# Slot selectors of a routing table: eight wide comparisons on VectorE in place of 64 narrow ones on GpSimd

## Chip, cores and metric

The kernel runs on one core of a Trainium2 chip. The metric is the device time of one execution in microseconds (us); for the kernel before, three runs gave 2314.49, 2322.72 and 2324.0 us, so the median is 2322.72 us.

## The reference

Input x has 4096 tokens of 256 features, all float32. Two layers follow each other; each adds an attention-like part and a routed feed-forward part to the stream, both fed by the same layer norm:

```python
x = L0_attn_x
xn = _layernorm(x, axis=-1)
x = x + _L0_attn_ref(xn, ...) + _L0_ffn_ref(xn, ...)
xn = _layernorm(x, axis=-1)
x = x + _L1_attn_ref(xn, ...) + _L1_ffn_ref(xn, ...)
```

The change touches the second layer, in the stage that does its attention and the routing of its feed-forward part. The feed-forward part has 8 experts, and each token goes to the 2 with the highest scores, weighted by a softmax over the two:

```python
scores = jnp.einsum('bsd,ed->bse', x, Wg)
topk_scores, topk_idx = jax.lax.top_k(scores, k)
topk_probs = jax.nn.softmax(topk_scores, axis=-1)
h1 = jnp.einsum('bsd,efd->bsef', x, W1)
h2 = jnp.einsum('bsd,efd->bsef', x, W2)
hidden = jax.nn.silu(h1) * h2
expert_out = jnp.einsum('bsef,edf->bsed', hidden, W3)
...
return jnp.einsum('bse,bsed->bsd', gating, expert_out)
```

The attention part of that layer projects xn to q, k and v, normalizes each over all tokens (batch norm), takes a steep sigmoid of each, forms the 16x16 products v'v of each head, and multiplies q*k by them and by an output matrix.

## The kernel before

The program is a row of stages, each a block in which all engines have an instruction list of their own, with semaphores between them; at a block's end the engines meet. The stages are: the first norm, routing and state-space attention of layer 0, the experts of layer 0, the stage between the layers (`bridge_phase`, from line 1501), and the experts of layer 1 (`expert_phase`, called on line 2158). The last needs the lists that `bridge_phase` makes: for each of 72 tiles of 128 slots, sorted by expert, the token of each slot (`source`, `target`) and its weight (`gate`).

These lists are made by matrix products, without a scatter. There are 32 x 2 = 64 pairs of a token tile and a choice. For a pair, each of 128 tokens (on the partitions) has a tile `tile_f` (0 to 71) and a slot in that tile `slot_f` (0 to 127). The product of a 128x128 selector (1 where the column number is the token's slot) with a 128x144 load (token number, and weight, in the column of the token's tile) adds the tokens into the 128x144 `table`. The pairs are handled in 8 batches (`BATCHES`) of 8 pairs (`EB`). Selectors (`pick`) and loads (`loads`) have two buffers each, used in turn.

Who does what, and in which order:

- GpSimd makes the selectors in a loop at the end of its list (lines 1655 to 1663): eight comparisons of `slot_row` (0 to 127 along the columns) with one column of `slot_f` per batch, each 128x128. From batch 2 on it waits until the batch two before is multiplied (`s_tab`), and after each batch it raises `s_pick`.
- VectorE makes the loads in `load(m)` (lines 1953 to 1964) by three operations on 128x576 elements (lines 1959, 1962, 1964), each of which waits for the one ahead. `load(0)` and `load(1)` stand ahead of the loop, on both sides of `coefficients(0, K, 1)`, and `load(n + 2)` stands in step n of `v_step` (lines 1993 to 2008), for n from 0 to 5.
- TensorE's `v_step(n)` (lines 1733 to 1758): eight transposes of v (line 1740), in steps 0 and 1 also two more units of the projections (line 1674), then the wait for `s_pick` and `s_load`, the eight table products (line 1749), the wait for VectorE's copies of the transposed v (`s_vk`), and the eight v'v products (line 1756). Float32 matrix products stand twice in the profile's counts (x16 for eight).
- VectorE's `v_step(n)`: wait for the transposes, two copies out of PSUM (line 1997), in steps 0 to 3 four `bn_stats` (line 1870), in step 4 `moments` (lines 1969 to 1971), then `load(n + 2)`, an addition of a bias to the stream (line 2006), and in step 5 `coefficients(K, R, 2)` (lines 1977 to 1982), for which ScalarE waits before the sigmoids of k.
- ScalarE does the sigmoids (line 1831), of v, then q, then k.

After eight steps VectorE masks the v'v products (line 2013), TensorE forms the effective output matrix (line 1763), and the output loop (lines 1774, 2025, 2043) follows; then the experts begin. The expert stage gathers rows by `source` on GpSimd's queue (line 1286).

In the names of the rows below, `b_work` and `b_xn` are areas that several arrays share: the selectors lie in `b_work`, the loads of even batches in `b_work` and of odd ones in `b_xn`, and `tile_f`, `slot_f` in `b_xn`. `b_bank` is PSUM.

Of the kernel before, what the change touches and what calls it, by code (L numbers as in the profile page):

```python
# [7 lines left out]
ALU = mybir.AluOpType  # L8
# [4 lines left out]
P = 128  # L13
# [100 lines left out]
def bcast(ap, n):  # L114

    return ap.unsqueeze(2).to_broadcast([ap.shape[0], ap.shape[1], n])
# [1384 lines left out]
def bridge_phase(nc, sem, k, xs, y_dram, xnT, rows, w_small, w_qkv, w_p, bn_g, bn_b, bp, lists, etab, etab_dram, out, s_out, w13s, w2s):  # L1501
# [11 lines left out]
    e_n, k_n, nt = E1, K1, NT1  # L1513
    by_token = y_dram[SPARE:SPARE + S * K0, :].rearrange("(s k) d -> s (k d)", k=K0)
    with ctx:
# [27 lines left out]
        tile_f, slot_f = (spare[:, o:o + T * k_n].rearrange("p (t q) -> p t q", q=k_n) for o in (384, 448))  # L1543
        live = spare[:, 512:512 + nt]
        source, aimed, gate = lists
        EB = 8
        pick = work[:, 4096:4096 + 2 * EB * P].rearrange("p (r e s) -> p r e s", r=2, e=EB)
        loads = [b.rearrange("p (e a j) -> p e a j", e=EB, a=2)
                 for b in (work[:, 6144:6144 + EB * 2 * nt], spare[:, 640:640 + EB * 2 * nt])]
        slot_row_i, slot_row = sb("slot_row_i", [P, P], I32), sb("slot_row", [P, P])  # L1550
# [29 lines left out]
        s_rc, s_sel, s_pre, s_e, s_ex, s_rt = (sem("b_" + n) for n in (  # L1580
            "route_chain", "selected", "counted", "exp_in", "exp_out", "routed"))
        s_cz, s_iota, s_turn, s_pick, s_load, s_tab, s_et, s_etm = (sem("b_" + n) for n in (
            "comparisons_zeroed", "iotas", "iotas_turned", "slots_picked", "loads_set", "tabled", "expert_of_tile", "expert_moved"))
# [7 lines left out]
        BATCHES = T * k_n // EB  # L1591
# [8 lines left out]
        with nc.Block() as block:  # L1600
            @block.sync
            def _(sp):
                def y_half(h):
                    g, half = divmod(h, 2)
                    if g >= 2:
                        sp.wait_ge(s_x, g - 1)
                    sp.dma_start(yg[:, g % 2, half * 2:half * 2 + 2].rearrange("p t k d -> p t (k d)"),
                                 tokens(by_token, g * BIG + half * 2, 2)).then_inc(s_yg[h % 4], 16)

                for h in range(4):  # L1610
                    y_half(h)
                for g in range(NG):
                    if g + 2 < NG:
                        y_half(2 * g + 4)
                        y_half(2 * g + 5)
                    sp.wait_ge(s_xn, g + 1)
                    sp.dma_start(tokens(rows, g * BIG, BIG), xn[:, g % XN]).then_inc(s_row[g % XN], 16)
                sp.wait_ge(s_et, 1)
                sp.dma_start(etab_dram.rearrange("(c p) -> p c", p=P), etab_i[:], allow_slow_non_contiguous=True).then_inc(s_etm, 16)
                sp.wait_ge(s_etm, 16)  # L1620
                sp.dma_start(etab[:], etab_dram[0:nt].unsqueeze(0)).then_inc(s_etm, 16)
                for g in range(NG):
                    sp.wait_ge(s_xo, g + 1)
                    sp.dma_start(tokens(out, g * BIG, BIG), xs[:, g * BIG:(g + 1) * BIG, :]).then_inc(s_out, 16)
                for r in range(XN):
                    sp.wait_ge(s_row[r], len(range(r, NG, XN)) * 16)
                sp.wait_ge(s_etm, 32)

            @block.gpsimd
            def _(pool):  # L1630
                g_ = nc.gpsimd
                for h in range(2 * NG):
                    g, half = divmod(h, 2)
                    pool.wait_ge(s_yg[h % 4], (h // 4 + 1) * 16)
                    a = yg[:, g % 2, half * 2:half * 2 + 2]
                    g_.tensor_tensor(a[:, :, 0:2, :], a[:, :, 0:2, :], a[:, :, 2:4, :], ALU.add).then_inc(s_pc, 1)
                    pool.wait_ge(s_pc, h + 1)
                    g_.tensor_tensor(a[:, :, 0, :], a[:, :, 0, :], a[:, :, 1, :], ALU.add).then_inc(s_ys, 1)
                    if h == 1:
                        g_.iota(tokid[:], pattern=[[P, T]], base=-S, channel_multiplier=1).then_inc(s_iota, 1)  # L1640
                        g_.iota(ji[:], pattern=[[1, 1]], base=0, channel_multiplier=1).then_inc(s_iota, 1)
                        g_.iota(slot_row_i[:], pattern=[[1, P]], base=0, channel_multiplier=0).then_inc(s_iota, 1)
                        pool.wait_ge(s_iota, 3)
                        g_.tensor_copy(token_f[:], tokid[:]).then_inc(s_turn, 1)
                        g_.tensor_copy(jf[:], ji[:]).then_inc(s_turn, 1)
                        g_.tensor_copy(slot_row[:], slot_row_i[:]).then_inc(s_turn, 1)
                pool.wait_ge(s_x, NG - 1)
                g_.memset(cmp, 0.0).then_inc(s_cz, 1)
                g_.memset(mask[:], 1.0).then_inc(s_m, 1)
                m3 = mask[:].rearrange("p (h d) -> p h d", d=HD)  # L1650
                for n, (op, low, sign) in enumerate(((ALU.is_ge, 0, 1), (ALU.is_ge, HD - 1, -1))):
                    pool.wait_ge(s_m, n + 1)
                    g_.affine_select(out=m3, in_=m3, compare_op=op, fill=0.0, base=low,
                                     pattern=[[-sign * HD, P // HD], [0, HD]], channel_multiplier=sign).then_inc(s_m, 1)
                pool.wait_ge(s_rt, 1)
                pool.wait_ge(s_turn, 3)
                for n in range(BATCHES):
                    if n >= 2:
                        pool.wait_ge(s_tab, n - 1)
                    for x in range(EB):  # L1660
                        t, q = divmod(n * EB + x, k_n)
                        ins = g_.tensor_scalar(pick[:, n % 2, x, :], slot_row[:], slot_f[:, t, q:q + 1], None, ALU.is_equal)
                    ins.then_inc(s_pick, 1)

            @block.tensor
            def _(pe):
                mm = nc.tensor.matmul
# [181 lines left out]
            def _(dve):  # L1849
                v = nc.vector  # L1850
# [72 lines left out]
                for e in range(e_n):  # L1923
                    ins = v.tensor_tensor_scan(incl[:, :, e], k["ones"][:, 0:T], tot[:, :, e], 0.0, ALU.mult, ALU.add)
# [28 lines left out]
                def load(m):  # L1953
                    at = slice(m * EB // k_n, (m + 1) * EB // k_n)
                    half = lambda a: loads[m % 2][:, :, a, :].rearrange("p (t q) j -> p t q j", q=k_n)
                    wide = lambda ap: ap.unsqueeze(3).to_broadcast([P, EB // k_n, k_n, nt])
                    if m >= 2:
                        dve.wait_ge(s_tab, m - 1)
                    v.tensor_tensor(half(0), slot_row[:, 0:nt].unsqueeze(1).unsqueeze(1).to_broadcast([P, EB // k_n, k_n, nt]),
                                    wide(tile_f[:, at, :]), ALU.is_equal).then_inc(s_load, 1)  # L1960
                    dve.wait_ge(s_load, 3 * m + 1)
                    v.tensor_tensor(half(1), half(0), wide(gates[:, at, :]), ALU.mult).then_inc(s_load, 1)
                    dve.wait_ge(s_load, 3 * m + 2)
                    v.tensor_tensor(half(0), half(0), wide(bcast(token_f[:, at], k_n)), ALU.mult).then_inc(s_load, 1)
# [20 lines left out]
                for n in AFTER[:8]:  # L1985
                    unit(n)
                moments(0, K, FULL)
                load(0)
                dve.wait_ge(s_nb, 4)
                coefficients(0, K, 1)  # L1990
                load(1)

                def v_step(s):
                    reached(dve, s_vt, s)
                    reached(dve, s_vv, s, 2)
                    for b in range(2):
                        ins = v.tensor_copy(vt[:, s.slot(2), 2 * b:2 * b + 2, :].rearrange("p u d -> p (u d)"), v_ps[b][:])
                    ins.then_inc(s_vk, 1)
                    for n in AFTER[8 + 4 * s.n:12 + 4 * s.n]:
                        unit(n)  # L2000
                    if s.n == 4:
                        moments(K, R, UNITS)
                    if s.n + 2 < BATCHES:
                        load(s.n + 2)
                    part = xs[:, s.n * BIG:(s.n + 1) * BIG, :]
                    v.tensor_tensor(part, part, middle(bp[:], BIG), ALU.add).then_inc(s_bp, 1)
                    if s.n == 5:
                        coefficients(K, R, 2)
# [3 lines left out]
                for c in range(KD):  # L2012
                    ins = v.scalar_tensor_tensor(vv[:, c, :], v_sum[c][:, 0:P], SCALE, mask[:], ALU.mult, ALU.mult)
# [15 lines left out]
                for c in range(KD):  # L2029
                    ins = v.tensor_copy(weff[:, c, :], bank[6 + c][:, 0:D])  # L2030
# [18 lines left out]
def program(nc, x, w_proj, b_proj, b_dt, conv_w, dt_bias, a_log, d_col, norm_col, w_out, b_out,  # L2049
# [11 lines left out]
    with ExitStack() as top:  # L2061
# [89 lines left out]
        with Semaphores(nc, sem) as own:  # L2151
            bridge_phase(nc, own, k, xs, y0, xnT, rows, wsm1, wqkv, wp, g_sb, b_sb, bp_sb, lists1, etab1, etabs[1], out, s_out, w13s, w2s)
# [49 lines left out]
```

## Time and profile before

| what | value |
|---|---|
| median of three runs | 2322.72 us (2314.49 to 2324.0) |
| time of the profiled execution | 2307.0 us |
| its span in the trace | 2305.1 us |
| mean granted TensorE clock | 0.985 |
| busy: TensorE / VectorE / ScalarE / GpSimd | 93% / 68% / 52% / 62% |
| the stage of the change, from the first copies of `v_step` to the last v'v product | 1777.58 to 1829.17 us, 51.6 us |
| GpSimd's selectors | 64 comparisons, first at 1758.8 us, last at 1824.5 us |

The profile is that of one execution, and its times are microseconds from the start of the span. A timeline row gives the start, the time to the end of its last instruction, engine, line, operation and tiles, the count, and in brackets how long the engine was idle ahead of it and what ended that. The time between two rows' starts is what an engine really takes for the first of them, since the end of one instruction overlaps the start of the next by a little (0.07 us on VectorE).

### The profile page before, as it was taken

To read this page: it belongs to the slowest core of one execution; us is meant where nothing else is said; L and a number is where in the kernel's file an instruction comes from. 1 tells how busy PE (TensorE), PEld (TensorE's weight loads), DVE (VectorE), ACT (ScalarE), POOL (GpSimd) and SP (SyncE) were. 2 spreads that over 40 slices of the span, in tenths; PEclk is the share of its full clock that TensorE was granted. 3 is DMA by queue.
4 is the path that set the end of the run, shared out by engine and by line. 5 is a ranking of instruction groups with operands and counts; after the bars stand their busy time and mean duration, and the time that the engine had idled before them with its cause. 6 is when DMAs were issued, how large, how long until landed. Compare 5 with 4: busy or idle time off the path is not lost. (4 is left out here: it accounts for less than half of the span.)

```text
span 2305.1 us, 40600 instructions
## 1 busy us (share of the span) xinstructions
PE 2152.2 (93%) x12292; PEld 1574.2 (68%) x12292; DVE 1572.4 (68%) x3391; ACT 1205.1 (52%) x2706; POOL 1439.0 (62%) x1272
## 2 busy tenths in 40 slices
PE   4878999999999999999999989999799889999997
PEld 2446777777777777777777768788444756666664
DVE  5778888888888888888888865677596832222221
ACT  2456777777777777777777752222254511111111
POOL 1325777777777777777777766788672624444443
PEclk9989999999999999999999999999899999999999
DMA  9864445555445455544554527976450064222221
GB/s 323 320 145 115 138 146 151 152 143 145 143 138 147 138 142 148 155 139 143 147 155 140 147 72 239 296 244 198 173 212 10 19 219 128 46 46 44 45 43 19
DMA packets 193826, 329.02 MB, mean 143 GB/s; under 512 B 49235, under 2 KB 135508, under 8 KB 193364
## 3 DMA queue, kind: packets, MB, share of 16 engines
q1 hardware_dynamic: 137220, 232.12, 34.1%
q0 software_dynamic: 26880, 53.64, 9.0%
q10 hardware_dynamic: 29520, 40.66, 5.5%
q8 instruction: 110, 1.80, 0.3%
q14 instruction: 96, 0.79, 0.1%
HBM read 240.46 MB, written 86.79 MB: 142 GB/s over the span
## 5 line engine op out<-in xcount | busy, mean ns | idle before, releaser
L1014 DVE SCALAR_TENSOR_TENSOR m_cv<-m_hp,conv,m_cv 128x256 f32<-128x256 f32 x864 | 416.9, 482 | 112.2 <-ACT m_cv L913 91.0
L1405 PE MATMUL e_u<-wup,e_xgT 128*128 x1152 | 411.1, 490 | 0.5 <-DMA wdn<-in_w 0.5
L1343 ACT ACTIVATE e_sil<-e_u 128x128 f32<-128x128 f32 (+1 forms) x216 | 83.0, 384 | 523.7 <-PE e_u L1405 517.2
L840 POOL TENSOR_TENSOR m_er<-m_er,m_cT 128x1024 f32<-128x1024 f32 x128 | 302.2, 2361 | 45.4 <-DVE m_ar L1021 45.4
L951 ACT ACTIVATE m_ar<-m_ar,m_ta 128x128 f32<-128x128 f32 x1024 | 318.8, 391 | 0.8
L1102 PE MATMUL m_hp<-xnT,wpj 128*128 128x259 f32 x1152 | 304.7, 387 | 7.8 <-PEq L145 4.5
L1405 PEld LDWEIGHTS e_u<-wup,e_xgT 128*128 128x128 f32 x1152 | 203.9, 192 | 113.4 <-issue 105.5
L1110 PE MATMUL m_gp<-xnT,wpj 128*128 128x256 f32 x1024 | 268.3, 384 | 11.2 <-ACT m_gT L931 11.1
L1102 PEld LDWEIGHTS m_hp<-xnT,wpj 128*128 128x128 f32 x1152 | 214.2, 192 | 68.8 <-issue 27.4
L1300 POOL DMA_INDIRECT out<-e_y,target x72 | 113.0, 1570 | 228.5 <-DVE e_y L1374 194.6
L847 POOL TENSOR_TENSOR m_hdd<-m_hdt,m_tb 128x512 f32<-128x512 f32 x128 | 131.0, 1043 | 193.4 <-DVE m_hdt L1029 193.4
L1161 PE MATMUL m_out<-wo,m_gT 128*128 128x256 f32 x1024 | 242.9, 380 | 0.0
L931 ACT ACTIVATE m_gT<-m_gp,bias 128x256 f32<-128x256 f32 x256 | 121.4, 474 | 230.8 <-PE m_gp L1110 230.8
L1367 DVE SCALAR_TENSOR_TENSOR e_hid<-e_sil,gate,e_u 128x512 f32<-128x512 f32 x72 | 53.8, 747 | 254.4 <-ACT e_sil L1343 254.4
L1161 PEld LDWEIGHTS m_out<-wo,m_gT 128*128 128x128 f32 x1024 | 193.0, 190 | 47.8 <-issue 23.9
L1424 PE MATMUL e_d<-wdn,e_hidT 128*128 x864 | 224.3, 382 | 1.0 <-DVE e_y L1374 1.0
L1110 PEld LDWEIGHTS m_gp<-xnT,wpj 128*128 128x128 f32 x1024 | 178.1, 190 | 35.7 <-ACT m_gT L931 19.0
L881 POOL DMA_INDIRECT rows_by_slot<-m_xrow,posi x128 | 171.5, 1340 | 32.8 <-issue 28.0
L913 ACT ACTIVATE m_cv<-m_hp,m_bsum,conv 128x256 f32<-128x256 f32 x288 | 160.4, 557 | 55.2 <-PE m_hp L1102 53.8
L1308 POOL DMA_INDIRECT y_rows<-e_y,e_target x144 | 145.5, 1010 | 46.9 <-DVE e_y L1374 34.8
L1424 PEld LDWEIGHTS e_d<-wdn,e_hidT 128*128 128x128 f32 x864 | 147.1, 190 | 23.7 <-issue 1.8
L1047 DVE SCALAR_TENSOR_TENSOR m_y<-m_hT,dcol,m_yt 128x128 f32<-128x128 f32 x512 | 143.2, 342 | 23.5 <-PE m_yt L1150 23.5
(326 smaller groups left out, 3927.7 us busy)
## 6 DMA issues: line engine op xcount, KB each, us to landing
m_ar<-acum_rows_dram SPq DMA_DIRECT2D x512, 128.0 KB, 3.9
m_er<-eacum_rows_dram SPq DMA_DIRECT2D x128, 512.0 KB, 4.4
rows_by_slot<-blank_rows ACTq DMA_DIRECT2D x1, 18576.0 KB, 81.4
e_xg<-rows_by_slot ACTq DMA_DIRECT2D x132, 129.0 KB, 3.4
m_xrow<-xn_rows SPq DMA_DIRECT2D x32, 512.0 KB, 5.0
b_work<-y_rows SPq DMA_DIRECT2D x16, 1024.0 KB, 7.0
wup<-in_w SPq DMA_DIRECT2D x8, 1024.0 KB, 5.4
wpj<-in_w_proj SPq DMA_DIRECT2D x1, 4352.0 KB, 23.6
```

The costliest lines, as they stand in the source:

```text
L840: g.tensor_tensor(er[:, t], er[:, t], middle(cT[:, t * P:(t + 1) * P], HQ), ALU.mult).then_inc(scaled.sem, 1)
L881: pool.indirect_dma_start(by_slot, bass.IndirectOffsetOnAxis(posi[:, i * TB + t, r:r + 1], 0), xrow[:, t, r, :], None).then_inc(s_scat[t], 16)
L913: a(cv[:, n % 6, :], hp[n % 2][:, OLD:PW], ACT.Identity, bias=bsum[:, c:c + 1], scale=conv[:, c, OLD:TAPS]).then_inc(heva.sem, 1)
L951: ins = a(row, row, ACT.Exp, bias=ta[:, t, q * HQ + h:q * HQ + h + 1])
L1014: v_.scalar_tensor_tensor(o, hp[n % 2][:, j:j + BLK], conv[:, c, j:j + 1], o, ALU.mult, ALU.add).then_inc(tapped.sem, 1)
L1047: ins = v_.scalar_tensor_tensor(y1[:, cols], hT[:, conv_of(cc), t * P:(t + 1) * P], d_col[:, cc:cc + 1], yt[s % 2][:, cols], ALU.mult, ALU ...
L1102: ins = mm(hp[n % 2][:, 0:PW], w_proj[:, kd, col:col + P], xpad[:, kd, ds(i * BLK, PW)], start=kd == 0, stop=kd == KD - 1)
L1110: ins = mm(gp[:, 0:BLK], w_proj[:, kd, cc * P:(cc + 1) * P], xpad[:, kd, ds(i * BLK + OLD, BLK)], start=kd == 0, stop=kd == KD - 1)
L1161: ins = mm(out_ps[:, t * D:(t + 1) * D], gT[:, q % 2 * CQ + c, t * P:(t + 1) * P], w_out[:, cc, :], start=s == 0 and c == 0, stop=cc == CH ...
L1308: pool.indirect_dma_start(y_dram, bass.IndirectOffsetOnAxis(row_of(n), 0), y[:, n % YR, :], None).then_inc(s_y[n % YR], 16)
L1405: ins = nc.tensor.matmul(u_ps[a.slot(2)][b][:, 0:width], xgT[:, a.slot(2), c, :], wup[:, c, ds(e * (2 * f) + b * width, width)], start=c = ...
L1424: ins = nc.tensor.matmul(d_ps[d.slot(2)][:, 0:D], hidT[:, d.slot(2), c * P:(c + 1) * P], wdown[:, ds(e * (FC * D) + c * D, D)], start=c == ...
```

## The change

GpSimd's loop is removed, with its waits for `s_rt` and `s_turn`. VectorE's `load(m)` gets one operation more, ahead of its three and behind its wait for `s_tab`: all eight selectors of the batch in one comparison of 128x1024 elements, with `slot_row` broadcast over the pairs and `slot_f` over the columns. It raises `s_pick`; nothing on VectorE waits for it.

```diff
-                pool.wait_ge(s_rt, 1)
-                pool.wait_ge(s_turn, 3)
-                for n in range(BATCHES):
-                    if n >= 2:
-                        pool.wait_ge(s_tab, n - 1)
-                    for x in range(EB):
-                        t, q = divmod(n * EB + x, k_n)
-                        ins = g_.tensor_scalar(pick[:, n % 2, x, :], slot_row[:], slot_f[:, t, q:q + 1], None, ALU.is_equal)
-                    ins.then_inc(s_pick, 1)
-
             @block.tensor
...
                     if m >= 2:
                         dve.wait_ge(s_tab, m - 1)
+                    v.tensor_tensor(pick[:, m % 2].rearrange("p (t q) s -> p t q s", q=k_n),
+                                    slot_row[:].unsqueeze(1).unsqueeze(1).to_broadcast([P, EB // k_n, k_n, P]),
+                                    slot_f[:, at, :].unsqueeze(3).to_broadcast([P, EB // k_n, k_n, P]), ALU.is_equal).then_inc(s_pick, 1)
                     v.tensor_tensor(half(0), slot_row[:, 0:nt].unsqueeze(1).unsqueeze(1).to_broadcast([P, EB // k_n, k_n, nt]),
                                     wide(tile_f[:, at, :]), ALU.is_equal).then_inc(s_load, 1)
```

Line numbers behind the removed loop fall by 10 up to `load`, and by 7 behind the added lines.

On GpSimd, at the end of its list for this stage (the rows behind are those of the block's end and of the expert stage), the difference is:

```order
 L1649 MEMSET b_mask 128x128
 L1653 AFFINE_SELECT b_mask<-b_mask 128x128 x2
-L1662 TENSOR_SCALAR b_work<-b_slot_row,b_xn 128x128 x64
 L1600 UNCONDITIONAL_BRANCH
 L1280 UNCONDITIONAL_BRANCH
```

The 64 comparisons are gone, and nothing of GpSimd's stands behind the mask in this stage.

On VectorE, from the copies of step 1 of `v_step` to those of step 2, the kernel before has:

```order
L1997 COPY b_work<-b_bank 128x512 x2
L1870 BN_STATS b_stats<-xnT 128x6 x4
L1959 TENSOR_TENSOR b_xn<-b_slot_row,b_xn 128x8x72
L1962 TENSOR_TENSOR b_xn<-b_xn 128x8x72
L1964 TENSOR_TENSOR b_xn<-b_xn,b_token_f 128x8x72
L2006 TENSOR_TENSOR xs<-xs,bp_sb 128x1024
L1997 COPY b_work<-b_bank 128x512 x2
```

and the changed one:

```order
L1990 COPY b_work<-b_bank 128x512 x2
L1860 BN_STATS b_stats<-xnT 128x6 x4
L1949 TENSOR_TENSOR b_work<-b_slot_row,b_xn 128x1024
L1952 TENSOR_TENSOR b_xn<-b_slot_row,b_xn 128x8x72
L1955 TENSOR_TENSOR b_xn<-b_xn 128x8x72
L1957 TENSOR_TENSOR b_xn<-b_xn,b_token_f 128x8x72
L1999 TENSOR_TENSOR xs<-xs,bp_sb 128x1024
L1990 COPY b_work<-b_bank 128x512 x2
```

The wide comparison stands between the `bn_stats` and the load, so every later copy on VectorE stands behind one comparison more. All eight calls of `load` have this form.

## Rows read from the trace of the kernel before

**Rows 1.** The page: busy time by engine, and the chain that ended last.
```profile
PE 2152.2 (93%) x12292; PEld 1574.2 (68%) x12292; DVE 1572.4 (68%) x3391; ACT 1205.1 (52%) x2706; POOL 1439.0 (62%) x1272
PE e_u L1405 11%; PE e_d L1424 5%; PE e_h_ps L1416 1%; PE e_x_ps L1394 1%; DMA e_xg<-xn_rows,source 0%; DMA out<-e_y,target 0%; POOL out L1300 0%; DVE e_xgT L1359 0%; DVE e_y L1374 0%; POOLq L1300 0%; POOLq L1299 0%; POOLq L1324 0%; POOLq L145 0%
```
**Rows 2.** Waits from 1776 to 1830: in total, times, longest (us).
```profile
DVE b_work L1997 <- PE b_bank L1740: 7.4, 2, 5.5
PE b_bank L1756 <- DVE b_work L1997: 3.7, 4, 2.2
PE b_bank L1749 <- POOL b_work L1662: 1.4, 2, 1.0
ACT xnT L1831 <- DVEq L1983: 0.9, 1, 0.9
```
**Rows 3.** Timeline of TensorE, steps 2 to 7 of `v_step`.
```profile
1795.86 2.05 PE L1756 MATMUL b_bank<-b_work 128*128 128x128 f32 x16 [0.25 <-DVE b_work L1997]
1797.75 1.04 PE L1740 MATMUL b_bank<-ident,b_raw 128*128 128x128 f32 x8
...
1802.93 3.17 PE L1756 MATMUL b_bank<-b_work 128*128 128x128 f32 x16 [2.17 <-DVE b_work L1997]
1805.89 1.61 PE L1740 MATMUL b_bank<-ident,b_raw 128*128 128x128 f32 x8
...
1821.82 2.05 PE L1756 MATMUL b_bank<-b_work 128*128 128x128 f32 x16
...
1825.16 2.23 PE L1749 MATMUL b_bank<-b_xn,b_work 128*128 128x144 f32 x16 [0.42 <-POOL b_work L1662]
1827.22 1.95 PE L1756 MATMUL b_bank<-b_work 128*128 128x128 f32 x16
```
**Rows 4.** Timeline of VectorE, steps 2, 3 and 6 of `v_step`.
```profile
1794.53 1.28 DVE L1997 COPY b_work<-b_bank 128x512 f32<-128x512 f32 x2
1795.73 2.46 DVE L1870 BATCH_NORM_STATS2 b_stats<-xnT 128x6 f32<-128x512 f32 x4
1798.11 0.74 DVE L1959 TENSOR_TENSOR b_work<-b_slot_row,b_xn 128x576 f32<-128x576 f32 x1
1798.89 0.81 DVE L1962 TENSOR_TENSOR b_work<-b_work,b_xn 128x576 f32<-128x576 f32 x1
...
1800.46 1.21 DVE L2006 TENSOR_TENSOR xs<-xs,bp_sb 128x1024 f32<-128x1024 f32 x1
1801.60 1.28 DVE L1997 COPY b_work<-b_bank 128x512 f32<-128x512 f32 x2
...
1820.47 1.29 DVE L1997 COPY b_work<-b_bank 128x512 f32<-128x512 f32 x2 [0.21 <-DVE b_a_b L1982]
```
**Rows 5.** Timeline of VectorE: end of the first coefficients, `load(1)`, the starts of `load(2)` and `load(3)`.
```profile
1769.42 0.16 DVE L1982 TENSOR_TENSOR b_a_b<-b_a_b,b_std 128x4 f32<-128x4 f32 x1
1769.73 0.76 DVE L1959 TENSOR_TENSOR b_xn<-b_slot_row,b_xn 128x576 f32<-128x576 f32 x1
1770.53 0.76 DVE L1962 TENSOR_TENSOR b_xn<-b_xn 128x576 f32<-128x576 f32 x1
...
1782.97 0.76 DVE L1959 TENSOR_TENSOR b_work<-b_slot_row,b_xn 128x576 f32<-128x576 f32 x1 [1.73 <-PE b_bank L1749]
...
1791.03 0.76 DVE L1959 TENSOR_TENSOR b_xn<-b_slot_row,b_xn 128x576 f32<-128x576 f32 x1 [0.89 <-PE b_bank L1749]
```
**Rows 6.** Timeline of ScalarE: the first sigmoids of v.
```profile
1774.87 1.52 ACT L1831 ACTIVATE b_raw<-b_raw,b_a_b,b_a_s 128x512 f32<-128x512 f32 x2
```
**Rows 7.** GpSimd's comparisons, line 1662 (min/median/max ns).
```profile
L1662 POOL TENSOR_SCALAR b_work<-b_slot_row,b_xn x64: 592/598/1918, 1758.8 to 1824.5; 128x128 f32<-128x128 f32 x64
```
**Rows 8.** Timeline of GpSimd: its last 40 comparisons.
```profile
1791.09 34.02 POOL L1662 TENSOR_SCALAR b_work<-b_slot_row,b_xn 128x128 f32<-128x128 f32 x40 [1.25 <-PE b_bank L1749]
```
**Rows 9.** Stretches: PE, PEld, DVE, ACT, POOL busy, granted clock, DMA share, GB/s.
```profile
1794.00:1830.00 36.00, 30.25 (x231) 28.51 (x230) 31.23 (x52) 25.60 (x36) 31.10 (x38) 0.95 0.00 1
1803.80:1807.20 3.40, 3.40 (x18) 3.40 (x18) 3.33 (x6) 0.00 (x0) 3.40 (x5) 0.52 0.02 5
```

## The prediction, made before the changed kernel ran

> **What bounds the kernel now.** I read the page first, then the waits of the stage of the change, then the timelines of its engines. On the page [rows 1] the reader is to see that TensorE is busy for 93% of the span, and that the chain that ended last runs through the last expert stage. That chain does not reach the change, so it says nothing of what the change costs. The link is the order of the program: the expert stage starts only when all engines have ended the stage ahead, and those lists are its input. So a microsecond by which the loop of eight steps ends later is a microsecond of the whole, unless something covers it.
>
> In that loop the waits [rows 2] show who is late. TensorE waited four times for VectorE's copies, 3.7 us in all, and twice for GpSimd's selectors, 1.4 us in all. The timelines show the cadence: in steps 2 and 3 VectorE's copies start at 1794.53 and 1801.60 [rows 4], 7.07 us apart with no idle in between. TensorE needs, from its v'v products of step 6 to those of step 7, 1827.22 - 1821.82 = 5.40 us with a wait of 0.42, so 4.98 us of work a step [rows 3]. VectorE therefore bounds steps 2 to 5, not GpSimd; TensorE has 2 us of slack a step. The stretch says the same: from 1794 to 1830 VectorE is busy 31.23 of 36 us, TensorE 30.25 [rows 9]. The change takes work off the engine that waits and gives it to the one that bounds.
>
> **The price of a comparison.** The trace has no such operation on 1024 columns, but two neighbours. The bias addition (line 2006) has the same size, type and engine and one broadcast operand: from its start to the next copy's, 1801.60 - 1800.46 = 1.14 us [rows 4]. The line 1959 is the same operation with the same two broadcasts on 576 elements: 0.76 us [rows 5]. The lower end is those 0.76 us, since a larger operation of the same form should not be shorter; the upper end scales it by size, 0.76 x 1024 / 576 = 1.35 us. I take 1.14, the row of equal size.
>
> **Comparisons 0 and 1.** They stand ahead of the loop. Behind number 0 come the first coefficients, which end at 1769.42 + 0.16 = 1769.58 [rows 5]; ScalarE starts the sigmoids that need them at 1774.87 [rows 6], so 1.14 us fits 4 times over. Both together are 2.3 us, and VectorE then waits up to 5.5 us for the first transposes [rows 2]. Cost 0; what hides them is the row of projections ahead of step 0. Without that cover they would cost 2.3 us.
>
> **Comparisons 2 and 3.** `load(2)` starts when table batch 0 is multiplied, at 1782.97, before and after. Then two comparisons push the copies of step 2, less the 0.89 us that VectorE idled ahead of `load(3)` [rows 5], as it will arrive late there: 2 x 1.14 - 0.89 = 1.4 us. TensorE followed VectorE by a wait of 0.25 us there [rows 3], so it moves along.
>
> **Comparisons 4 to 7.** They stand in steps 2 to 5, where VectorE has no idle worth counting: 4 x 1.14 = 4.6 us. So the copies of step 6, which ended at 1820.47 + 1.29 = 1821.76 [rows 4], end 1.4 + 4.6 = 6.0 us later. Steps 6 and 7 have no load, and TensorE bounds from there to 1827.22 + 1.95 = 1829.17 [rows 3].
>
> **What is given back.** The 64 comparisons of GpSimd cost nothing of their own, except where TensorE waited for them: 0.42 us ahead of the last batch [rows 3] is behind the copies of step 6, and goes, -0.4. The other wait, 1.0 us, lies ahead of those copies and is covered by them. The second thing is crowding. `load(1)` ran with GpSimd idle, and its second operation took 0.76 us; the same with GpSimd at work took 0.81 [rows 4, 5]. So two of a load's three operations gain 0.05 us: 6 loads x 0.1 = -0.6.
>
> The Trainium skill (SBUF — State Buffer, Who interferes with whom) goes much further: a VectorE instruction with two SBUF inputs and a GpSimd one that reads SBUF exclude each other, and the later one is blocked until the other ends. By that page VectorE could gain up to a whole GpSimd operation at each of its four such instructions a batch, in place of 0.1 us. The trace bears out who pays: it is GpSimd, whose comparisons took 0.598 us at the median [rows 7] but 34.02 / 40 = 0.85 us each in the crowded stretch [rows 8].
>
> **Others waiting.** The second coefficients stand behind `load(7)` and move by about 5.8 us. ScalarE waited 0.9 us for them [rows 2], then has 16 sigmoids of k in a row; the output loop takes two of these per step of 3.5 us and starts itself 5 us later, so nothing comes of it. SP has no issue inside the loop. GpSimd reaches the block's end early and waits there.
>
> **The sum.** 0 + 1.4 + 4.6 - 0.4 - 0.6 = **+5.0 us**. The profiled execution took 2307.0 us, so by its own time 2312.0; it lies 15.7 us under the median of the three runs, and the difference is put on the median: 2322.7 + 5.0 = **2327.7 us**, 0.2% more. A measurement of this kernel can tell about 0.5%, 11.6 us, from no change, so I forecast a kernel that is slower by too little to see.
>
> **TensorE's clock** is the open term. Waiting for VectorE 2.17 us ahead of the v'v products of step 3 was followed by a fall to the lower level: granted clock 0.52 from 1803.8 to 1807.2 [rows 9], the 1.2 GHz level. It stretched the products from 2.05 to 3.17 us and the transposes from 1.04 to 1.61 [rows 3], 1.7 us in all, hidden then by VectorE's pace. Waits of 0.25 and 0.42 us were followed by none. With the change VectorE's steps take 8.1 us (7.07 + 1.14 - 0.1) against TensorE's 5.0, so it waits some 3 us in each of steps 3 and 4, and 2.3 us ahead of step 6. Falls in the first two are hidden: 5.0 + 1.7 is under 8.1. A fall at step 6 or behind it is not, and costs 1.7 us. The wait at step 6 is near the one row that had a fall; I give it somewhat less than even odds, since it stands alone, and leave it out of the likeliest time.
>
> **The rivals.**
>
> *A, the clock becomes the bound (slower).* At the lower level a step of TensorE takes twice 4.98, 10.0 us, more than VectorE's 8.1. If the waits keep the clock there from step 3 to the end, TensorE starts the products of step 3 at 1805.3 (1802.93 + 1.4 + 1.0), and four steps of 10.0 us and the last products at 3.9 follow: about 1849, 20 us past 1829.17, and 2343 us. It decides when more than 6 of a step's 8.1 us run at the lower level; below that VectorE hides it. For it speak the longer waits; against it, that the fall after 2.17 us of wait was over in 3.4 us with work resumed [rows 9]. The Trainium skill (TensorE: Matmul & The Clock Gate, HAM oscillation) describes exactly this, bursts of matmuls between waits that each start at the lower clock; here the one fall agrees, and one fall is not a stage. Chance 0.07.
>
> *B, VectorE is freed (as fast or faster).* If GpSimd held up VectorE in ways that durations don't show, the change would give back more than it takes. The ceiling is what TensorE lost from 1794 to 1830, 36 - 30.25 = 5.8 us of idle, with 1.7 us for the clock: 7.5 us, so not below 2315 us, still within 0.5%. With a gain of one comparison of 0.6 us at four instructions a step it would be 1.3 us less a step over four steps, 5 us less in all: 2318. Against it speaks that VectorE's load started its operations 0.78 us apart beside GpSimd [rows 4] and 0.80 us apart without it [rows 5]. Chance 0.04.
>
> *C, the comparison is covered or cheap.* At 0.76 us each, 2 x 0.76 - 0.89 + 4 x 0.76 - 1.0 = 2.7 us: 2325. Chance 0.10. At the upper end of 1.35 us it is 2 x 1.35 - 0.89 + 4 x 1.35 - 1.0 = 6.2 us, 2329, which belongs to the forecast.
>
> *D, the forecast with exposed falls.* One or two falls at 1.7 us behind step 6: +6.7 to +8.4, 2329 to 2331. Chance 0.34. The forecast itself, +4 to +6.2 us, has 0.45.
>
> **How the numbers follow.** All cases but A lie within 0.5% of 2322.7. The runs of the kernel before spread over 9.5 us, and the profiled execution is 7.5 us below the lowest of them, so scatter is larger than the effect and starts 5 us off centre: I put 0.09 of it above the bound and 0.02 below. That makes faster 0.02, same 0.82, slower 0.07 + 0.09 = 0.16. For the range I take the forecast from the lowest run, 2314.5 - 2 (under C and B), and the upper end just under A's 2343, which leaves less than 2 in 10 outside: 2312 to 2342.
>
> **What would show it.** The new rows on VectorE should be x8, 128x1024, 1.2 us each. The copies of `v_step` should start 8.1 us apart in steps 2 to 4 in place of 7.07, TensorE's wait for them should rise from 3.7 to about 12 us, and its waits for GpSimd be gone. The last v'v product should end near 1834.2 against 1829.17 (as far as the span runs alike ahead of it), and the stages behind should have their old lengths. A comparison well off 1.2 us, copies still 7 us apart, or a granted clock near 0.5 over most of the loop would make the sum wrong; a difference outside the loop would make the reading wrong that only the loop is touched.

## The result and the profile after

The changed kernel takes 2328.91 us, the median of 12 runs (2321.99 to 2332.73); the kernel before, beside it, 2321.85 us (2314.49 to 2324.93). The ratio is 1.0026, with a 95% interval of 1.0014 to 1.0038: 6.0 us more (2321.85 x 0.0026), between 3.3 and 8.8. The two medians themselves lie 7.1 us apart, inside that interval. It is slower by an amount that lies under the 0.5% set ahead, and that twelve runs can still tell from nothing.

The page of the kernel after (busy time by engine) shows little of it beside [rows 1]:

```profile
PE 2162.0 (93%) x12292; PEld 1577.3 (68%) x12292; DVE 1583.9 (68%) x3399; ACT 1206.0 (52%) x2706; POOL 1387.0 (60%) x1208
```

VectorE gained 8 instructions and 11.5 us of busy time, GpSimd lost 64 and 52 us. The waits from 1780 to 1850 answer to [rows 2]:

```profile
PE b_bank L1746 <- DVE b_work L1990: 10.1, 5, 3.2
DVE b_work L1990 <- PE b_bank L1730: 5.7, 2, 3.8
ACT xnT L1821 <- DVEq L1976: 2.9, 1, 2.9
```

TensorE's wait for VectorE's copies rose from 3.7 to 10.1 us, its wait for GpSimd's selectors is gone, and VectorE's idle ahead of step 0 shrank from 5.5 to 3.8 us, which is where most of comparisons 0 and 1 went (1.7 of their 2.3 us; a wait of 0.22 us for ScalarE and shorter operations around them took the rest). The 10.1 us are less than the 12 that were forecast because the fall of the clock in step 3 kept TensorE busy longer and so shortened its next wait to 1.56 us. ScalarE waits 2.9 us for the second coefficients in place of 0.9, and nobody waits for the sigmoids behind them. The timeline of TensorE, after (first transposes; the products of steps 2, 3 and 6; the last three steps of the loop; the output loop), against [rows 3]:

```profile
1792.71 1.09 PE L1730 MATMUL b_bank<-ident,b_raw 128*128 128x128 f32 x8 [0.57 <-ACT b_raw L1821]
...
1813.20 2.05 PE L1746 MATMUL b_bank<-b_work 128*128 128x128 f32 x16 [1.33 <-DVE b_work L1990]
...
1821.29 2.75 PE L1746 MATMUL b_bank<-b_work 128*128 128x128 f32 x16 [3.20 <-DVE b_work L1990]
1823.84 1.92 PE L1730 MATMUL b_bank<-ident,b_raw 128*128 128x128 f32 x8
...
1843.15 2.05 PE L1746 MATMUL b_bank<-b_work 128*128 128x128 f32 x16 [2.20 <-DVE b_work L1990]
...
1845.91 2.13 PE L1739 MATMUL b_bank<-b_xn,b_work 128*128 128x144 f32 x16
1847.88 1.95 PE L1746 MATMUL b_bank<-b_work 128*128 128x128 f32 x16
...
1852.89 29.58 PE L1764 MATMUL b_bank<-b_weff,b_raw 128*128 128x256 f32 x128 [1.35 <-DVE b_weff L2023]
```

And the timeline of VectorE, after, from the copies of step 2 to those of step 3, and the copies of step 6, against [rows 4]:

```profile
1811.87 1.28 DVE L1990 COPY b_work<-b_bank 128x512 f32<-128x512 f32 x2
...
1815.45 1.21 DVE L1949 TENSOR_TENSOR b_work<-b_slot_row,b_xn 128x1024 f32<-128x1024 f32 x1
1816.57 0.75 DVE L1952 TENSOR_TENSOR b_work<-b_slot_row,b_xn 128x576 f32<-128x576 f32 x1
1817.36 0.76 DVE L1955 TENSOR_TENSOR b_work<-b_work,b_xn 128x576 f32<-128x576 f32 x1
...
1819.96 1.28 DVE L1990 COPY b_work<-b_bank 128x512 f32<-128x512 f32 x2
...
1841.81 1.29 DVE L1990 COPY b_work<-b_bank 128x512 f32<-128x512 f32 x2 [0.21 <-DVE b_a_b L1975]
```

The new row is 1.21 us long and takes 1816.57 - 1815.45 = 1.12 us of VectorE's way. The copies are 1819.96 - 1811.87 = 8.09 us apart, where they were 7.07.

The absolute times differ by more than that: the first transposes stand at 1792.71 after and at 1776.44 before. So everything below is measured from marks inside the stage. They are TensorE's products that count the tokens (line 1729 before, 1719 after), the first transposes, the end of the last v'v product (the loop lies between these two), and the start and end of the output loop. Before, in the first trace, the marks that stand in no row ahead are:

```profile
1747.37 0.59 PE L1729 MATMUL b_bank<-b_work,before 128*128 128x256 f32 x2
...
1776.44 1.09 PE L1740 MATMUL b_bank<-ident,b_raw 128*128 128x128 f32 x8 [0.57 <-ACT b_raw L1831]
...
1832.23 27.89 PE L1774 MATMUL b_bank<-b_weff,b_raw 128*128 128x256 f32 x128 [1.35 <-DVE b_weff L2030]
```

and after:

```profile
1763.63 0.59 PE L1719 MATMUL b_bank<-b_work,before 128*128 128x256 f32 x2
```

Read so, for all kernels of this study (us; between loop and output loop lie 3.1 us in every trace):

| kernel | count to first transposes | loop | output loop | from the count to the end | against before |
|---|---|---|---|---|---|
| before | 29.07 | 52.73 | 27.89 | 112.75 | |
| before, again | 29.08 | 52.71 | 27.89 | 112.74 | 0.0 |
| after | 29.08 | 57.12 | 29.58 | 118.84 | +6.1 |
| after, again | 29.08 | 58.79 | 27.89 | 118.82 | +6.1 |
| extra comparison beside GpSimd's | 29.07 | 57.92 | 27.89 | 117.94 | +5.2 |
| two comparisons | 29.09 | 63.92 | 29.58 | 125.64 | +12.9 |
| after, bias additions on GpSimd | 35.02 | 52.81 | 27.89 | 118.78 | +6.0 |
| selectors split, bias on GpSimd | 35.37 | 50.02 | 29.58 | 118.02 | +5.3 |
| selectors split, bias kept clear | 29.09 | 49.05 | 27.89 | 109.09 | -3.7 |
| after, bias kept clear | 29.09 | 52.53 | 27.89 | 112.57 | -0.2 |

The change costs 6.1 us there: 4.4 in the loop and 1.7 in the output loop. What follows the output loop is the same in both first traces, 2305.1 - 1860.12 = 445.0 us before and 2327.3 - 1882.47 = 444.8 after. The other 16.3 us between the two traces lie ahead of the count, where the change touches nothing.

### The profile page after: what moved, and what is told of

The parts are those of the page before. It is cut to its first block and busy times, and to the rows that moved or that the text cites. A ratio compares the mean times of both kernels' runs of the same rounds, so it can differ in the third digit from the quotient of the medians.

```text
span 2327.3 us, 40543 instructions
## 1 busy us (share of the span) xinstructions
PE 2162.0 (93%) x12292; PEld 1577.3 (68%) x12292; DVE 1583.9 (68%) x3399; ACT 1206.0 (52%) x2706; POOL 1387.0 (60%) x1208
## 5 line engine op out<-in xcount | busy, mean ns | idle before, releaser
L1286 POOL DMA_INDIRECT e_xg<-xn_rows,source x72 | 71.3, 990 | 169.3 <-POOLq L145 147.6
```

## The experiments

**Two more traces: is what lies ahead of the count scatter?** Both kernels unchanged, each once more.

> The kernel before once more, for a second trace. Its counting products stood at 1747 us in the first trace, and at 1758 to 1764 in those of after and of the four experiments. If that is scatter of the stages ahead, this trace has them there too, and the lengths from there on are those of the first: 29.1 and 52.7 us, output loop 27.9. If the change made the stages ahead longer, it has them near 1747 again.

> The kernel after once more. Loop 57.1 us again. The output loop took 29.58 us in the first trace, with a fall of the clock in it, against 27.89 before: if the fall follows from the waits of the loop it is there again; if it is chance, it may be absent.

The kernel before took 2318.3 us, and its counting products now stand at 1759.09, not 1747:

```profile
1759.09 0.59 PE L1729 MATMUL b_bank<-b_work,before 128*128 128x256 f32 x2
1788.17 1.09 PE L1740 MATMUL b_bank<-ident,b_raw 128*128 128x128 f32 x8 [0.57 <-ACT b_raw L1831]
...
1838.93 1.95 PE L1756 MATMUL b_bank<-b_work 128*128 128x128 f32 x16
...
1843.94 27.89 PE L1774 MATMUL b_bank<-b_weff,b_raw 128*128 128x256 f32 x128 [1.36 <-DVE b_weff L2030]
```

So 11.7 us between two executions of the same kernel lie ahead of the count, and from there on they agree within 0.02 us. The second trace of the kernel after, below, has its count at 1757.85, 5.8 us ahead of its first. The 16.3 us are thus of the size of the scatter between executions, and the trace shown first was a quick one. The kernel after, again, took 2323.84 us; its extra time is the same 6.1 us, but lies elsewhere:

```profile
1815.50 2.05 PE L1746 MATMUL b_bank<-b_work 128*128 128x128 f32 x16 [3.20 <-DVE b_work L1990]
...
1823.60 3.28 PE L1746 MATMUL b_bank<-b_work 128*128 128x128 f32 x16 [3.21 <-DVE b_work L1990]
...
1837.41 3.43 PE L1746 MATMUL b_bank<-b_work 128*128 128x128 f32 x16 [2.25 <-DVE b_work L1990]
1840.63 1.34 PE L1730 MATMUL b_bank<-ident,b_raw 128*128 128x128 f32 x8
...
1848.78 27.89 PE L1764 MATMUL b_bank<-b_weff,b_raw 128*128 128x256 f32 x128 [1.35 <-DVE b_weff L2023]
```

The products of step 6, behind a wait of 2.25 us, took 3.43 us in place of 2.05: the fall of the clock that came in the output loop in the first trace came here inside the loop, which is 1.7 us longer for it (58.79 against 57.12), and the output loop is back at 27.89.

**An extra comparison, GpSimd left as it was.** The kernel before, with the new operation on VectorE writing to memory that nothing reads:

```diff
+                    v.tensor_tensor(spare[:, 1792:2816].rearrange("p (t q s) -> p t q s", q=k_n, s=P),
+                                    ..., ALU.is_equal)
                     v.tensor_tensor(half(0), slot_row[:, 0:nt]...
```

> The kernel before, with the wide comparison added on VectorE (its result goes to unused memory); GpSimd still makes the selectors. The loop is measured from the first transposes of v_step to the end of the last v'v product: 52.7 us before, 57.1 after. Theory 1 (VectorE bounds the loop; the change costs what its comparisons cost, less 1.0 us that the idle GpSimd gives back): loop 57.7 us, run about 6 us over before. Rival (the loss comes from moving work off GpSimd, for example from semaphores or where the selectors come from, and the comparison itself is covered): loop within 1 us of 52.7. If GpSimd's absence gives back nothing, the loop is 57.1 as after.

Measured: 2327.29 us beside 2320.93, ratio 1.0027 (1.0016 to 1.0037); loop 57.92. VectorE's timeline, steps 2 and 3:

```profile
1809.74 1.27 DVE L2000 COPY b_work<-b_bank 128x512 f32<-128x512 f32 x2
...
1813.32 1.20 DVE L1959 TENSOR_TENSOR b_xn<-b_slot_row,b_xn 128x1024 f32<-128x1024 f32 x1
1814.45 0.74 DVE L1962 TENSOR_TENSOR b_work<-b_slot_row,b_xn 128x576 f32<-128x576 f32 x1
...
1817.88 1.28 DVE L2000 COPY b_work<-b_bank 128x512 f32<-128x512 f32 x2
```

The loss is there with GpSimd's comparisons still made and still used. So it is VectorE's length, not the move off GpSimd: the rival of the covered comparison is out. TensorE waits for GpSimd nowhere in this loop either, since it comes later itself and finds the selectors ready. What GpSimd's silence gives back beyond those waits is 57.92 - 57.12 = 0.8 us, 0.7 of it ahead of the copies of step 6; 0.6 was expected. The clock fell in steps 3 and 5, and VectorE's pace hid both falls.

**Two comparisons in each load.** The kernel after, with the same unused comparison behind the new one.

> The kernel after, with the wide comparison made twice in each load (the second result goes to unused memory). Theory 1: six more on the path, none of them with idle to swallow it, 6 x 1.14 = 6.8 us: loop 63.9 us, copies of v_step 9.2 us apart, first two still hidden in the 3.8 us of idle ahead of step 0; run about 14 us over before, plus 1.7 us if a clock fall is exposed. Rival (the clock: TensorE in the longer waits stays at the lower level and bounds the loop): loop over 67 us and granted clock near 0.5 in most of it. Rival (comparison covered): loop 57 us.

Measured: 2334.62 us, ratio 1.0059 (1.0045 to 1.0073); loop 63.92 us, 6.80 over the 57.12 of after, and one fall of the clock in the output loop, 29.58. VectorE's copies and TensorE's products:

```profile
1817.73 1.28 DVE L1993 COPY b_work<-b_bank 128x512 f32<-128x512 f32 x2
...
1826.95 1.28 DVE L1993 COPY b_work<-b_bank 128x512 f32<-128x512 f32 x2
```
```profile
1809.84 3.61 PE L1746 MATMUL b_bank<-b_work 128*128 128x128 f32 x16 [3.60 <-DVE b_work L1993]
...
1819.07 2.98 PE L1746 MATMUL b_bank<-b_work 128*128 128x128 f32 x16 [2.78 <-DVE b_work L1993]
...
1836.10 2.95 PE L1746 MATMUL b_bank<-b_work 128*128 128x128 f32 x16 [2.92 <-DVE b_work L1993]
```

The clock fell in steps 2, 3 and 5, and the loop is still as long as VectorE's work says: 6.80 us more for six comparisons, priced at 6.84. TensorE's waits for the copies rose to 13.7 us in all, from 10.1. The rival in which the clock becomes the bound is out even with two comparisons in each load.

**The bias additions on GpSimd.** If VectorE's length is the cause, taking the same length from it must give the loss back. The kernel after, with this on GpSimd, behind the mask, and line 1999 gone:

```diff
+                pool.wait_ge(s_rt, 1)
+                pool.wait_ge(s_x, NG)
+                pool.wait_ge(s_xn, NG)
+                for g in range(NG):
+                    part = xs[:, g * BIG:(g + 1) * BIG, :]
+                    g_.tensor_tensor(part, part, middle(bp[:], BIG), ALU.add).then_inc(s_bp, 1)
```

> The kernel after, with the eight bias additions taken from VectorE's steps and done by GpSimd, in a row, as soon as the routing chain is over. Theory 1: six additions of 1.14 us leave VectorE's way, about 1 us of that turns into idle ahead of the third load: loop 51.4 to 52.4 us, about 5 us under after and 0 to 1 us under before; copies 7.0 us apart. Rival (the loss of the change is not VectorE's length): loop stays at 57. Rival (GpSimd's additions crowd VectorE's chain while they run, 8 x 2.36 us from 1759 on): the first transposes come later by more than 1 us, measured from the end of the routing chain.

Measured: 2327.82 us, ratio 1.003 (1.002 to 1.004): no gain, though the loop fell to 52.81. What it won it lost ahead of the loop, where the first transposes came 35.02 us after the count in place of 29.1. VectorE's and GpSimd's timelines, and TensorE's first transposes:

```profile
1770.82 4.84 DVE L1867 BATCH_NORM_STATS2 b_stats<-b_raw 128x6 f32<-128x512 f32 x8
...
1777.54 3.22 DVE L1956 TENSOR_TENSOR b_work<-b_slot_row,b_xn 128x1024 f32<-128x1024 f32 x1
1780.68 2.91 DVE L1959 TENSOR_TENSOR b_work<-b_slot_row,b_xn 128x576 f32<-128x576 f32 x1
1783.63 2.80 DVE L1962 TENSOR_TENSOR b_work<-b_work,b_xn 128x576 f32<-128x576 f32 x1
1786.46 2.78 DVE L1964 TENSOR_TENSOR b_work<-b_work,b_token_f 128x576 f32<-128x576 f32 x1
```
```profile
1770.35 21.09 POOL L1660 TENSOR_TENSOR xs<-xs,bp_sb 128x1024 f32<-128x1024 f32 x8 [36.72 <-DVEq L1943]
```
```profile
1793.92 1.97 PE L1737 MATMUL b_bank<-ident,b_raw 128*128 128x128 f32 x8 [6.52 <-ACT b_raw L1828]
```

Beside GpSimd's additions each of these VectorE operations, which have two inputs in SBUF, took 2.8 to 3.2 us in place of 0.76 to 1.2. That is 2.0 to 2.2 us longer, somewhat less than one addition of GpSimd (2.37 us at the median where nothing collides, in the split run below with the additions kept clear; 21.09 / 8 = 2.64 us here). The `bn_stats`, with one input, kept their 4.84 us for eight. The first coefficients stand behind that load, and ScalarE and TensorE waited for them. The Trainium skill (SBUF — State Buffer, Who interferes with whom) says that such a VectorE instruction and a GpSimd one that reads SBUF exclude each other; by that page this is what must happen, and the trace agrees. The recorded rival was right and the main expectation wrong.

**Selectors split.** VectorE makes those of batches 0 and 1, which cost it nothing, GpSimd the additions and then batches 2 to 7:

```diff
+                for g in range(NG):
+                    ... bias addition g on GpSimd
...
-                for n in range(BATCHES):
-                    if n >= 2:
-                        pool.wait_ge(s_tab, n - 1)
+                pool.wait_ge(s_pick, 2)
+                for n in range(2, BATCHES):
+                    pool.wait_ge(s_tab, n - 1)
...
+                    if m < 2:
+                        ... the wide comparison on VectorE
```

> VectorE makes the selectors of batches 0 and 1 alone (wide, where it has cover), GpSimd does the bias additions in that time and then the selectors of batches 2 to 7 in narrow comparisons as before. Theory 1: VectorE's steps take 5.9 us and nothing else is near: loop 47 to 48 us, run 5 us under before, 12 under after. Rival (GpSimd becomes the bound, with its comparisons at the crowded 0.85 us: 6.8 us a batch): loop 50 to 52 us, waits of TensorE for line 1662 of several us, run 1 to 2 us under before.

Measured: 2326.25 us, ratio 1.0016 (1.0005 to 1.0026). The loop is 50.02 us, but the first transposes came at 35.37, by the same collision, and the clock was low for them and for the projections behind (granted clock 0.60 from 1797 to 1805). Neither expectation held as a whole: the loop is as long as the rival said, but TensorE waited only 0.3 us for GpSimd, and the run is not faster than before.

**The same two, with the additions kept clear.** Five additions on GpSimd: two while VectorE runs its eight `bn_stats` and `moments`, three behind `load(1)`, when VectorE has nothing to do or operations with one input. Steps 5 to 7 keep theirs on VectorE:

```diff
+                pool.wait_ge(s_et, 1)
+                for g in range(5):
+                    if g == 2:
+                        pool.wait_ge(s_load, 6)
+                    ... bias addition g on GpSimd
...
+                    if s.n >= 5:
                         ... bias addition of step n on VectorE
```

With the selectors split:

> VectorE makes the selectors of batches 0 and 1, GpSimd those of 2 to 7, as in the split run; but GpSimd does only five of the eight bias additions, two after the routing chain while VectorE runs bn_stats, three after load(1), so that none lies beside an operation of VectorE with two inputs in SBUF. Steps 5 to 7 keep theirs on VectorE. If the port is the cause of the late first transposes: they come 29.1 us after the counting products again (35 in the two runs with all eight additions in a row), and VectorE's operations of load(0) take 0.75 us, not 2.9. Loop about 49 us (the split run's 50.0, less some 2 us of low clock at its start, plus 1.1 us for the addition in step 5), so 3 to 4 us under before in all. If additions on GpSimd hold up VectorE whatever it runs: the first transposes stay at 33 us or more.

With all selectors on VectorE:

> The kernel after (all selectors on VectorE) with the same five bias additions on GpSimd at the same places. Theory: first transposes at 29.1 us; copies of v_step 7.0 us apart in steps 2 and 3; loop 52.5 us, that is the loop of before within half a us, since the additions taken away are worth what the comparisons cost. Run within 2 us of before. If the loss of the change had another cause than VectorE's length, the loop would stay near 57.

The second came out as 2320.89 us, ratio 0.9997 (0.9988 to 1.0006), loop 52.53. The start of VectorE's `load(3)`, then its copies of steps 2 and 3:

```profile
1806.78 1.22 DVE L1958 TENSOR_TENSOR b_work<-b_slot_row,b_xn 128x1024 f32<-128x1024 f32 x1 [0.99 <-PE b_bank L1748]
...
1810.18 1.28 DVE L1999 COPY b_work<-b_bank 128x512 f32<-128x512 f32 x2
...
1817.13 1.28 DVE L1999 COPY b_work<-b_bank 128x512 f32<-128x512 f32 x2
```

The copies are 6.95 us apart again. Five additions of 1.14 us left VectorE's way, 0.99 us of that became idle, and the loop is 57.12 - 52.53 = 4.59 us shorter: the comparisons' cost is given back by taking a like length off VectorE, with the selectors still made there. The first gave 2318.07 us beside 2321.13, ratio 0.9984 (0.9974 to 0.9993), faster than both kernels by more than its uncertainty, loop 49.05. VectorE in `load(0)`, then GpSimd, then TensorE at the marks and where GpSimd now comes late:

```profile
1782.74 0.75 DVE L1970 TENSOR_TENSOR b_work<-b_slot_row,b_xn 128x576 f32<-128x576 f32 x1
1783.53 0.76 DVE L1973 TENSOR_TENSOR b_work<-b_work,b_xn 128x576 f32<-128x576 f32 x1
```
```profile
1775.58 4.68 POOL L1664 TENSOR_TENSOR xs<-xs,bp_sb 128x1024 f32<-128x1024 f32 x2 [37.30 <-DVE b_etab_i L1957]
1789.87 7.01 POOL L1664 TENSOR_TENSOR xs<-xs,bp_sb 128x1024 f32<-128x1024 f32 x3 [9.62 <-DVE b_xn L1975]
...
1807.11 30.34 POOL L1669 TENSOR_SCALAR b_work<-b_slot_row,b_xn 128x128 f32<-128x128 f32 x40 [2.31 <-PE b_bank L1756]
```
```profile
1792.47 1.09 PE L1747 MATMUL b_bank<-ident,b_raw 128*128 128x128 f32 x8 [0.57 <-ACT b_raw L1838]
...
1831.91 2.23 PE L1756 MATMUL b_bank<-b_work 128*128 128x144 f32 x16 [1.40 <-POOL b_work L1669]
...
1839.57 1.95 PE L1763 MATMUL b_bank<-b_work 128*128 128x128 f32 x16
```

The collision is gone. GpSimd's narrow comparisons, 30.34 / 40 = 0.76 us each, now hold TensorE up for 1.40 us in step 6 and 0.40 in step 7: they are the next thing that is late.

## Why the prediction held

- **The bound.** VectorE's steps set the loop, TensorE only follows: right. The copies are 8.09 us apart (forecast 8.1), and the double comparison lengthened the loop by 6.80 us (forecast 6.8).
- **The price of one comparison**, 1.14 us from the row of equal size: 1.12 to 1.15 measured, 6.80 for the six of the loop where 6.84 was forecast.
- **Comparisons 0 and 1 cost nothing**: right. The first transposes stand 29.08 us after the count, as before, and VectorE still waits 3.8 us there.
- **Comparisons 2 to 7 and what is given back by less crowding**: forecast 1.4 + 4.6 - 0.6 = 5.4 us at the copies of step 6. From the first transposes to those copies it is 1820.47 - 1776.44 = 44.03 us before and 1841.81 - 1792.71 = 49.10 after: 5.07, 0.3 less. The timelines show where. From the start of their first operation to the bias addition behind it, the six loads of the loop took 14.23 us before and, without the comparison, 13.52 after, so crowding was worth 0.7 us, not 0.6. The stretch from the `bn_stats` of step 1 to `load(3)` shrank from 3.35 to 2.38 us and so swallowed 0.97 us, not 0.89.
- **GpSimd's waits.** The 0.4 us behind step 6 was a little more. From the copies of step 6 to the loop's end it is 1829.17 - 1820.47 = 8.70 us before and 1849.83 - 1841.81 = 8.02 after, so 0.7. This wait cost more than the 0.42 us of idle that its row names: from the transposes of step 7 to the table products it was 1.46 us before and 0.87 after, 0.59 less, and the products ran a little longer before (2.23 against 2.13 us). In the extra-comparison run, where GpSimd still works, the same stretch is 0.87 us as well, so it was TensorE's later arrival that sufficed.
- **The loop** is thus 4.4 us longer, where the sum said 5.0.
- **The clock** was left out of the likeliest time, and this is the one choice that went the wrong way: both traces of the kernel after have one exposed fall, 1.7 us as priced, though not in the same place, and neither trace of the kernel before has one. The mechanism was case D's, +6.7 (0.34), rather than that of +5.0 (0.45). With 4.4 + 1.7 = 6.1 us the marks in the traces and the ratio of the runs (6.0 us) agree. That the longer waits cause the exposed fall is not shown: the extra-comparison run waited as long, up to 3.25 us, and had none.
- **Luck.** That the forecast time, 2327.7, lies only 1.2 us from the 2328.91 measured is in part chance. The median that it starts from was 0.9 us too high and the sum for the loop 0.6 us, against the 1.7 us of the clock that it left out.
- **Rivals.** A (the clock as the bound) is refuted by the double comparison. B (VectorE freed) found 0.7 us where its own price was 2.4 us a step, 9.6 over four steps. The evidence put against it was thin, as it compared the starts of a load's first two operations, which GpSimd hardly moved (0.78 and 0.80 us); the next start came after 0.84 us beside GpSimd and 0.79 without it. The mechanism itself is real, as the bias additions show, but the narrow comparisons hardly trigger it. C is refuted by the 1.12 us.
- **The runs** were thought to start 5 us off centre with a spread of 9.5 us. The median of before moved by 0.9 us with more runs, and the change was told from nothing at half of the bound that was set.

## What to carry to other kernels

Before work is moved between engines, find which of the two sets the pace of the stage, step by step: shares of the span (68% and 62% here) do not say it, a timeline without idle does. An operation that is shorter where it goes (1.12 us for 8 x 0.6) still costs its whole length if the engine that takes it is the one that is waited for, and nothing where that engine waits. GpSimd is a place for spare work only if its additions do not lie beside VectorE operations with two inputs in SBUF: eight of them in a row over 21 us put the first transposes off by 6 us, and five of them, placed in two groups of 12 us together, by nothing. A wait that is added on TensorE may also cost what the clock takes behind it, so price a fall (1.7 us here) and look whether another engine hides it.

## What was not expected of the hardware

- A `tensor_tensor` of GpSimd delayed a VectorE operation with two SBUF inputs by nearly its own length: 0.76 us became 2.8 to 2.9, where the addition alone takes 2.37. GpSimd's `tensor_scalar` on 128 columns, in a row without a gap, cost the same operation 0.05 us each (0.81 against 0.76) [rows 4, 5], and its own time rose instead, from 0.6 to 0.85 us. By the Trainium skill (SBUF — State Buffer, Who interferes with whom) the later of two such instructions is blocked until the other ends. The first case agrees; in the second VectorE lost far less than one comparison of 0.6 us. Why it is GpSimd that pays there was not tried.
- The same wait on the same engine does not always bring the lower clock. In the first trace of the kernel after, a wait of 3.20 us at step 3 was followed by a fall, in the second a wait of 3.20 us at that step was not, and one of 3.21 us at step 4 was. With the eight bias additions on GpSimd, TensorE waited 2.07 us twice in the loop and no fall followed. The granted clock by stretches in the first trace of after shows the exposed fall, at the start of the output loop, 9.7 us after the last wait of over 2 us (that at 1843.15) and right behind one of 1.35 us, which stands there before the change too, with no fall:

```profile
1852.80:1856.40 3.60, 3.51 (x9) 2.84 (x10) 1.17 (x2) 0.28 (x1) 0.00 (x0) 0.55 0.00 0
1856.40:1882.50 26.10, 26.07 (x121) 22.58 (x119) 15.82 (x20) 0.00 (x0) 0.00 (x0) 1.00 0.39 139
```

The columns are those of [rows 9]. What decides where a fall lands stays open. Its price was 1.7 us at each fall that lay in the open behind the loop or at its step 6. Ahead of the loop, where TensorE waited 6.5 and 6.9 us in the two runs with all eight additions on GpSimd, it was 1.4 and 2.7 us: from the first transposes to the first table products they took 5.78 and 7.07 us, against 4.37 elsewhere.
